# Projections of queries, keys and values as three passes over rounded and rest parts, in the causal and the self attention

## The chip, the cores and the metric

The kernel runs on one core of one Trainium2 chip. The metric is device time in microseconds (us) for one launch, the median of several runs; lower is better. TensorE (PE) multiplies matrices and writes to PSUM, VectorE (DVE) and ScalarE (ACT) compute element by element, GpSimd (POOL) does the same and issues DMAs, and SyncE (SP) issues DMAs.

## The reference

A decoder of two layers works on x, 4 sequences of 512 tokens and 256 features, in float32:

```python
x = x + _L0_attn_ref(_layernorm(x, axis=-1), ...)    # causal attention
x = x + _L0_xattn_ref(_layernorm(x, axis=-1), ctx_1024, ctx_1024, ctx_1024)   # gated gelu with the context
x = x + _L0_ffn_ref(_layernorm(x, axis=-1), ...)     # 8 experts, 2 a token, and a shared one
x = x + _L1_attn_ref(_layernorm(x, axis=-1), ...)    # self attention without a mask
x = x + _L1_xattn_ref(_layernorm(x, axis=-1), ctx_1024, ...)                  # cross attention
x = x + _L1_ffn_ref(_layernorm(x, axis=-1), ...)     # 8 experts, 2 a token
```

Each attention has 16 heads of 16 features. What the change touches is its first line:

```python
qkv = x @ W_attn.T + b_attn
q, k, v = jnp.split(qkv, 3, axis=-1)
```

The causal layer multiplies q and k by a factor of the position before the scores; the self attention of the second layer does not.

## The kernel before

The program runs five stages with a barrier between each: causal attention (names with `l0a`), gelu (`l0g`), experts (`l0m`), self attention followed by cross attention in one stage (`l1a`), experts (`l1m`). The change lies in `attention`, which both attention stages call.

`attention` works on batches (sequences) b = 0 to 3, and in `l1a` on 4 more of cross attention. A batch has 4 groups g of 4 heads, and a group has 8 steps j. One group is a slot (`self_slot`, L107). `attention_schedule` (L252) writes out a single list of steps for the whole stage, and each engine takes from the list the steps in which it has work, in that order. A step stands for an operation with a part on one or several engines:

- S: scores by key on PE (L959, and the mask at L929 in the causal layer), exponentials on ACT (L842). A: scores by query on PE (L920), row maxima on DVE (L729 causal, L734 self). Both share three PSUM buffers `s_ps` in turn, so PE waits when the reader of the buffer three turns back is not done.
- PV: probabilities by values on PE (L984). O, Z, N: the output of a group copied by ACT, turned by PE (L993), divided on DVE (L742, L746), turned back by PE (L1001) and copied by ACT (L859).
- M: row maxima turned by PE (L938) and copied by ACT (L811), for the group after.
- PREP with its EVAC, uses 0 to 7: the projections of the batch after, made one by one between the steps of this one. Uses 0 and 1 turn the normalised x (`xn`) with PE (L886), and ACT copies the result into `xnT` (L788). Uses 2 to 5 make the four 128-row chunks of queries and keys in the order `CHUNK` (L899), uses 6 and 7 the values (L906). Of queries and keys a rounded part `hi` and a rest `lo` are kept: the causal layer makes `qk` on DVE (L699), `hi` on ACT (L806) and `lo` on DVE (step LO, L716); the self attention makes both on DVE (L703, L705). ACT copies the values (L797).
- STACK, KEYS: DMAs that stack parts of `hi` and `lo` for the score products, issued by SP (L528), POOL (L608) and, for the first batch, ACT (L826).

Uses of later batches all go through one PSUM tile, `m_ps`, which N, M and the output projection (L1011) use too. `take_m` (L867) makes PE wait until whoever read `m_ps` last is done. For uses 0 and 1 this reader is named by `made` (L435): ACT's copy.

The first batch of a stage has nothing to hide behind. Its eight uses go through the three `s_ps` buffers ahead of the first slot, then the values and 8 A steps follow, and only then the first S:

```python
for use in range(8):
    yield "PREP", 0, use, 0
    yield "EVAC", 0, use, 0
    if 2 <= use < 6:
        yield "LO", 0, use, 0
    if use == 3:
        for g in range(2):
            yield "STACK", 0, g, 0
            yield from keys(0, g)
```

In the causal stage DVE's step LN2 of batch 0 ends with casts of constants, which wait for the DMAs of all seven constants (L678).

Of the kernel before, what the change touches and what calls it, by code (L numbers as in the profile page):

```python
# [19 lines left out]
F32 = mybir.dt.float32  # L20
# [8 lines left out]
P = 128  # L29
# [77 lines left out]
def self_slot(kinds, b, g):  # L107
# [12 lines left out]
    rests = {1: {0: 2, 2: 3}, 2: {2: 4, 5: 5}}.get(g, {})  # L120
    m_at = 5 if first else 3 if g in (1, 2) else 2
    turn_at = 5 if g == 0 else 6
# [172 lines left out]
def attention(nc, tag, x, const, stages):  # L295
# [12 lines left out]
    with ExitStack() as ctx:  # L308
# [18 lines left out]
        for n, (kind, w) in enumerate(stages):  # L327
            parts.append({"w": w, "kind": kind,
                          "wqkv": sb(f"wqkv{n}", [P, CC, 3 * D]), "wout": sb(f"wout{n}", [P, NG // 2, D]),
                          "bqk": sb(f"bqk{n}", [P, 2 * CC]), "bv": sb(f"bv{n}", [P, D]),  # L330
                          "bo": sb(f"bo{n}", [P, D]), "in": sem(f"w_in{n}")})

        def part(b):
            return parts[b // B]
# [4 lines left out]
        xn = sb("xn", [P, NT, D])  # L339
        xnT = sb("xnT", [P, CC, T])  # L340
        ctxT = sb("ctxT", [P, CC, T]) if has_cross else None
# [46 lines left out]
        m_act = steps("m_act", 4)  # L388
        m_dve = steps("m_dve", 4 if causal else 0)
        hi_done = steps("hi_done", 4)  # L390
        lo_done = steps("lo_done", 4)
# [102 lines left out]
        def in_stack(st, p, e, n):  # L494
            at = 64 * e + 16 * n
            return st[at:at + 16, p, :].bitcast(F32)

        block = ctx.enter_context(nc.Block())

        @block.sync  # L500
        def _(sp):
            def weights(n):
                w, at, loaded = parts[n]["w"], parts[n], parts[n]["in"]
                sp.dma_start(at["wqkv"][:, :, :], w["wqkv"].rearrange("(c p) n -> p c n", p=P)).then_inc(loaded, 16)
                sp.dma_start(at["bqk"][:, :], w["bqk"]).then_inc(loaded, 16)
# [61 lines left out]
        def _(pool):  # L567
            pool.memset(one_row[:, :].bitcast(F32), 1.0).then_inc(one_made, 1)

            def ln(b, *_):  # L570
# [13 lines left out]
                if b == 2 and has_cross:  # L584

                    w = parts[1]
                    pool.wait_ge(w["in"], 5 * 16)
                    for at in (w["wqkv"][:, :, 0:D], w["bqk"][:, 0:CC]):
                        pool.tensor_scalar(at, at, SCALE, None, ALU.mult).then_inc(q_scaled, 1)

            def bias(b, *_):

                if b % B == 0:
                    pool.wait_ge(part(b)["in"], 5 * 16)
                xn_done.wait(pool, b, NT - 1)
# [54 lines left out]
        def _(dve):  # L650
# [33 lines left out]
            def prep(b, use, _):  # L684
                if not 2 <= use < 6:
                    return
                if b % B == 0 and use == 2:

                    dve.wait_ge(part(b)["in"], 5 * 16)
                    if kinds[b] == "cross":  # L690
# [5 lines left out]
                if causal:  # L696
# [75 lines left out]
            def inverse_sums(b, g, kt):  # L772
                if kinds[b] != "cross":
# [5 lines left out]

            run({"LN1": ln, "LN2": normal, "EVAC": prep, "LO": rest, "ADD": out, "S": key_max, "W": inverse_sums,  # L780
                 "A": row_max, "Z": invert})

        @block.scalar
        def _(act):
            def prep(b, use, _):
                if use < 2:
                    m_ready.wait(act, b, use)
                    act.activation(xnT[:, use, :], product(b, use), ACT.Copy).then_inc(m_act.sem, 1)  # L788
                elif use >= 6:
# [9 lines left out]
                elif causal:  # L799
# [60 lines left out]

            run({"EVAC": prep, "S": exps, "O": copy_o, "M": negate_rows, "N": copy_back, "KEYS": first_stack})

        @block.tensor
        def _(pe):
            m_reader = [None]

            def take_m(steps, b, step):  # L867

                if m_reader[0]:
                    last, lb, lstep = m_reader[0]  # L870
                    last.wait(pe, lb, lstep)
                m_reader[0] = (steps, b, step)

            def prep(b, use, _):
# [13 lines left out]
                elif use < 6:  # L888
                    i = use - 2
                    if b % B == 0 and i == 0:  # L890
                        pe.wait_ge(w["in"], 5 * 16)
                        if cross:
                            pe.wait_ge(q_scaled, 2)
                    m_act.wait(pe, b, 1)
                    if cross and i == 1:
# [1484 lines left out]
```

## Time and profile before

| | |
|---|---|
| three runs | 1605.56, 1600.04, 1604.02 us, median 1604.02 |
| the profiled execution | 1612.28 us, of which the span from first to last instruction is 1610.5 |
| PE, matmuls | 1438.8 us busy, 89% of the span |
| DVE | 1176.1 us, 73% |
| ACT | 899.8 us, 56% |
| POOL | 612.2 us, 38% |
| causal attention | about 0 to 270 us of the span |
| self and cross attention | about 660 to 1190 us |

Busy time of PE counts from a matmul's start to its modelled end, and such spans overlap: what one matmul costs its successors is read from start to start. A float32 matmul appears as two records, a matmul of `float32r` operands (type F32R in the code) as one; the trace writes f32 for both. Numbers ahead of a row of the timeline are microseconds from the span's start.

### The profile page before, as it was taken

The numbers are of one execution on the slowest core, as the hardware profiler recorded it, in microseconds if no ns is written. First come the engines' busy times: TensorE is split into PE (matmuls) and PEld (weight loads), VectorE is DVE, ScalarE is ACT, GpSimd is POOL, SyncE is SP. The second block draws the span as 40 slices with busy tenths as digits, with TensorE's granted clock in tenths as the row PEclk, the third lists the DMA queues.
The fourth block names the chain that finished last, engine by engine and source line by source line (L and its number), as shares of the span: only waits on it lengthen the run. The fifth ranks groups of instructions, "written<-read, shape, count | busy, mean of one in ns | idle before, by whom it ended". The sixth has DMA issues, their size and how long they took to land. (4 is left out here: it accounts for less than half of the span.)

```text
span 1610.5 us, 30201 instructions
## 1 busy us (share of the span) xinstructions
PE 1438.8 (89%) x9918; PEld 994.5 (62%) x9918; DVE 1176.1 (73%) x2499; ACT 899.8 (56%) x1704; POOL 612.2 (38%) x881
## 2 busy tenths in 40 slices
PE   7899998989899999679999988999747899999996
PEld 3455554569899999333434333333236899999996
DVE  4776662554778888478878758988768688888883
ACT  1455553223256666036666687888814567776662
POOL 6445430010235654546445443553213223233311
PEclk8899998999999999769999999989978899999998
DMA  6223320130358886533223322232044678878772
GB/s 167 60 47 60 61 42 27 52 100 26 105 167 256 253 243 173 131 83 58 58 42 59 71 55 64 61 66 62 14 156 132 183 246 237 245 236 237 237 216 43
DMA packets 104553, 194.59 MB, mean 121 GB/s; under 512 B 30448, under 2 KB 55920, under 8 KB 101456
## 3 DMA queue, kind: packets, MB, share of 16 engines
q1 hardware_dynamic: 72016, 154.49, 30.8%
q0 software_dynamic: 31872, 37.79, 13.4%
q8 instruction: 79, 1.29, 0.3%
q14 instruction: 74, 0.61, 0.1%
q10 hardware_dynamic: 512, 0.40, 0.1%
HBM read 135.89 MB, written 18.61 MB: 96 GB/s over the span
## 5 line engine op out<-in xcount | busy, mean ns | idle before, releaser
L836 ACT ACTIVATE l1a_sb_probs<-l1a_s_ps,l1a_sb_kmax 128x512 f32<-128x512 f32 x256 | 172.4, 706 | 21.9 <-DVE l1a_sb_kmax L769 21.1
L734 DVE TENSOR_REDUCE l1a_sb_mx<-l1a_s_ps 128x2 f32<-128x1024 f32 x128 | 153.5, 1219 | 38.6 <-PE l1a_s_ps L920 38.5
L769 DVE TENSOR_REDUCE l1a_sb_kmax<-l1a_s_ps 128x1 f32<-128x512 f32 x256 | 161.0, 680 | 26.1 <-PE l1a_s_ps L959 25.2
L842 ACT ACTIVATE l1a_sb_probs<-l1a_s_ps 128x1024 f32<-128x1024 f32 x128 | 130.2, 1024 | 80.1 <-PE l1a_s_ps L959 79.9
L959 PEld LDWEIGHTS l1a_s_ps<-l1a_sb_qst,l1a_sb_kst 49*128 49x128 f32 (+1 forms) x512 | 49.1, 190 | 172.4 <-issue 95.3
L608 POOL DMA_DIRECT2D l1a_sb_kst<-l1a_sb_hi x228 | 112.9, 499 | 104.2 <-PE l1a_s_ps L959 96.2
L729 DVE CUSTOM_DVE_ANT_0 l0a_sb_seen<-l0a_s_ps,l0a_sb_above 128x128 f32<-128x128 f32 (+3 forms) x256 | 113.6, 488 | 52.5 <-PE l0a_s_ps L920 52.1
L2048 PE MATMUL l1m_g_ps<-l1m_sb_rows_hi,l1m_sb_hi 128*128 128x256 f32 x512 | 146.9, 287 | 1.1 <-DVE l1m_sb_late L1946 1.1
L959 PE MATMUL l1a_s_ps<-l1a_sb_qst,l1a_sb_kst 49*128 49x512 f32 (+1 forms) x512 | 127.5, 505 | 20.7 <-ACT l1a_sb_probs L836 18.9
L2048 PE MATMUL l1m_g_ps<-l1m_sb_rows_hi,l1m_sb_lo 128*128 128x256 f32 x512 | 145.3, 284 | 0.0
L2048 PE MATMUL l1m_g_ps<-l1m_sb_rows_lo,l1m_sb_hi 128*128 128x256 f32 x512 | 145.2, 284 | 0.0
L1781 POOL DMA_INDIRECT out_x<-l1m_sb_late,l1m_sb_add_to x39 | 64.9, 1663 | 192.2 <-DVE l1m_sb_late L1968 181.6
L1920 DVE TENSOR_TENSOR l1m_sb_lo<-l1m_sb_raw,l1m_sb_hi 128x512 fp32r<-128x512 f32 x184 | 119.8, 694 | 18.7 <-ACT l1m_sb_hi L1831 17.6
L842 ACT ACTIVATE l0a_sb_probs<-l0a_s_ps 128x1024 f32<-128x1024 f32 (+3 forms) x128 | 88.8, 702 | 63.7 <-PE l0a_s_ps L929 63.4
L2048 PE MATMUL l0m_g_ps<-l0m_sb_rows_hi,l0m_sb_hi 128*128 128x256 f32 x384 | 113.1, 294 | 7.1 <-DVE l0m_sb_rows_lo L1914 6.4
L2048 PE MATMUL l0m_g_ps<-l0m_sb_rows_hi,l0m_sb_lo 128*128 128x256 f32 x384 | 111.1, 289 | 0.0
L2048 PE MATMUL l0m_g_ps<-l0m_sb_rows_lo,l0m_sb_hi 128*128 128x256 f32 x384 | 111.1, 289 | 0.0
L1831 ACT ACTIVATE l1m_sb_hi<-l1m_sb_raw 128x512 fp32r<-128x512 f32 x184 | 104.9, 621 | 0.0
L2048 PE MATMUL l1m_y_ps<-l1m_sb_hi,l1m_sb_h_hi 128*128 128x256 f32 x312 | 91.9, 295 | 12.1 <-DVE l1m_sb_lo L1926 7.2
L2048 PEld LDWEIGHTS l1m_g_ps<-l1m_sb_rows_hi,l1m_sb_hi 128*128 128x128 f32 x512 | 98.8, 193 | 1.8 <-issue 1.5
L2048 PEld LDWEIGHTS l1m_g_ps<-l1m_sb_rows_hi,l1m_sb_lo 128*128 128x128 f32 x512 | 98.6, 193 | 0.1
L2048 PEld LDWEIGHTS l1m_g_ps<-l1m_sb_rows_lo,l1m_sb_hi 128*128 128x128 f32 x512 | 98.6, 193 | 0.0
(407 smaller groups left out, 3933.2 us busy)
## 6 DMA issues: line engine op xcount, KB each, us to landing
l1m_sb_raw<-in_l1m_w SPq DMA_DIRECT2D x92, 512.0 KB
l0m_sb_raw<-in_l0m_w SPq DMA_DIRECT2D x72, 512.0 KB
l1m_sb_raw<-in_l1m_w SPq DMA_DIRECT2D x23, 1024.0 KB
l1a_sb_qst<-l1a_sb_hi SPq DMA_DIRECT2D x256, 32.0 KB, 2.0
l1a_sb_kst<-l1a_sb_hi POOLq DMA_DIRECT2D x228, 32.0 KB, 2.0
l0a_sb_qst<-l0a_sb_hi SPq DMA_DIRECT2D x128, 32.0 KB, 2.3
l1a_sb_qst<-l1a_sb_lo SPq DMA_DIRECT2D x128, 32.0 KB, 2.1
l0a_sb_kst<-l0a_sb_hi POOLq DMA_DIRECT2D x124, 32.0 KB, 2.1
```

What stands on the lines that cost most here:

```text
L608: pool.dma_start(in_stack(kst, p, e, n), in_part(source, i, p, e)).then_inc(kstacked[p], 16)
L729: ins = dve.tensor_tensor_reduce(seen[:, j % 2, e, 0:last], buffer("A", b, g, j)[:, e, 0:last], above[:, T - last:T], 1.0, -3e38, ALU.add, ...
L734: dve.tensor_reduce(mx[:, g, qt, 2 * p:2 * p + 2], buffer("A", b, g, j)[:, :, :], AX.X, ALU.max).then_inc(a_max.sem, 1)
L769: dve.tensor_reduce(kmax[:, n % 4, e:e + 1], buffer("S", b, g, j)[:, e, :], AX.X, ALU.max, negate=True).then_inc(kmax_done.sem, 1)
L836: ins = act.activation(probs[:, n % 8, e, :], at[:, e, :], ACT.Exp, bias=kmax[:, n % 4, e:e + 1], accum_out=zsum[:, n % 4, e:e + 1])
L842: act.activation(probs[:, n % 8, :, c0:T], at[:, :, c0:T], ACT.Exp, scale=SCALE).then_inc(exp_done.sem, 1)
L959: ins = pe.matmul(at[:, e, c0:T], kst[rows, p, kt * P:(kt + 1) * P], qst[rows, p, c0:T], start=True, stop=not causal)
L1781: pool.indirect_dma_start(total, bass.IndirectOffsetOnAxis(ap=at, axis=0), y[:, e % 2, t, :], None, compute_op=ALU.add).then_inc(stored[e ...
L1831: ins = act.activation(two_chunks(hi, s % 2, f), raw13[:, s % n13, f, n, :, :], ACT.Copy)
L1920: ins = dve.tensor_tensor(two_chunks(lo, s % 2, f), raw13[:, s % n13, f, n, :, :], two_chunks(hi, s % 2, f).bitcast(F32), ALU.subtract)
L2048: ins = pe.matmul(at, s, m, start=n == 0, stop=n == len(passes) - 1)
```

## The change

The normalised and turned x is kept as a rounded part `x_hi` (ACT, in place of the copy into `xnT`) and a rest `x_lo` (DVE, a new step XLO). The weights of the causal and of the self attention are split once a stage into `w_hi` (ACT) and `w_lo` (DVE), in three pieces (step SPLIT: half of the query and key columns, the other half, the value columns). Each float32 product of these two layers becomes three float32r passes (hi by hi, lo by hi, hi by lo). Cross attention stays as it was. The weights' DMA gets a semaphore of its own. The reader of `m_ps` after uses 0 and 1 is now XLO instead of ACT's copy, and M moves from step 2 to step 3 in the slots of group 0.

```diff
-    m_at = 5 if first else 3 if g in (1, 2) else 2
+    turned_rests = {0: {4: 0, 5: 1} if first else {2: 0, 6: 1}}.get(g, {})
+    m_at = 5 if first else 2 if g == 3 else 3
@@
     for j in range(2 * NT):
         yield "S", b, g, j
+        if nxt is not None and kinds[nxt] != "cross" and j in turned_rests:
+            yield "XLO", nxt, turned_rests[j], 0
@@ def attention_schedule(kinds):
     yield "LN1", 0, 0, 0
     yield "LN2", 0, 0, 0
+    yield "SPLIT", 0, 0, 0
     for use in range(8):
         yield "PREP", 0, use, 0
         yield "EVAC", 0, use, 0
+        if use < 2:
+            yield "XLO", 0, use, 0
+        if use in (1, 4):
+            yield "SPLIT", 0, (use + 2) // 3, 0
         if 2 <= use < 6:
             yield "LO", 0, use, 0
@@ def made(b, use):
+            if use < 2 and kinds[b] != "cross":
+                return x_rest, b, use
@@ vector
+            def split_rest(_, k, __):
+                dve.wait_ge(w_split, k + 1)
+                dve.tensor_tensor(columns(w_lo, k), columns(parts[0]["wqkv"], k), columns(w_hi, k).bitcast(F32),
+                                  ALU.subtract).then_inc(w_rest, 1)
+
+            def turned_rest(b, use, _):
+                m_act.wait(dve, b, use)
+                v_ready.wait(dve, b - 1, 1)
+                dve.tensor_tensor(x_lo[:, use, :], product(b, use), x_hi[:, use, :].bitcast(F32), ALU.subtract
+                                  ).then_inc(x_rest.sem, 1)
@@ scalar
-                    act.activation(xnT[:, use, :], product(b, use), ACT.Copy).then_inc(m_act.sem, 1)
+                    at = xnT if kinds[b] == "cross" else x_hi
+                    act.activation(at[:, use, :], product(b, use), ACT.Copy).then_inc(m_act.sem, 1)
+            def split_weights(_, k, __):
+                act.wait_ge(parts[0]["wqkv_in"], 16)
+                act.activation(columns(w_hi, k), columns(parts[0]["wqkv"], k), ACT.Copy).then_inc(w_split, 1)
@@ tensor
+            def three_passes(at, chunks):
+                passes = [(s[a], m[b]) for s, m in chunks for a, b in ((0, 0), (1, 0), (0, 1))]
+                for n, (s, m) in enumerate(passes):
+                    ins = pe.matmul(at, s, m, start=n == 0, stop=n == len(passes) - 1)
+                return ins
@@ uses 2 to 5
+                    if not cross:
+                        if b == 0:
+                            pe.wait_ge(w_rest, 1 + i // 2)
+                        x_rest.wait(pe, b, 1)
+                        cols = slice(CHUNK[i] * P, (CHUNK[i] + 1) * P)
+                        ins = three_passes(at, [((w_hi[:, c, cols], w_lo[:, c, cols]), (x_hi[:, c, :], x_lo[:, c, :]))
+                                                for c in range(CC)])
@@ uses 6 and 7
+                    if b == 0:
+                        pe.wait_ge(w_rest, 3)
...
+                        if not cross:
+                            ins = three_passes(cols, [((x_hi[:, c, rows], x_lo[:, c, rows]),
+                                                       (w_hi[:, c, 2 * D:3 * D], w_lo[:, c, 2 * D:3 * D]))
+                                                      for c in range(CC)])
```

What DVE does for the first batch of the causal stage, before, from the end of LN2 to the first of the A steps (a row names line, operation, what is written and read, the shape, and how many follow):

```order
L682 CAST const_span_b<-l0a_sb_span 128x256
L699 SCALAR_TENSOR_TENSOR l0a_sb_qk<-l0a_s_ps,l0a_sb_bqk,const_rope 128x512
L716 TENSOR_TENSOR l0a_sb_lo<-l0a_sb_qk,l0a_sb_hi 128x512
L699 SCALAR_TENSOR_TENSOR l0a_sb_qk<-l0a_s_ps,l0a_sb_bqk,const_rope 128x512
L716 TENSOR_TENSOR l0a_sb_lo<-l0a_sb_qk,l0a_sb_hi 128x512
```

And in the changed kernel, whose line numbers are its own:

```order
L703 CAST const_span_b<-l0a_sb_span 128x256
L731 TENSOR_TENSOR l0a_sb_w_lo<-l0a_sb_wqkv,l0a_sb_w_hi 128x2x2x128
L737 TENSOR_TENSOR l0a_sb_x_lo<-l0a_s_ps,l0a_sb_x_hi 128x512 x2
L731 TENSOR_TENSOR l0a_sb_w_lo<-l0a_sb_wqkv,l0a_sb_w_hi 128x2x2x128
L720 SCALAR_TENSOR_TENSOR l0a_sb_qk<-l0a_s_ps,l0a_sb_bqk,const_rope 128x512
L748 TENSOR_TENSOR l0a_sb_lo<-l0a_sb_qk,l0a_sb_hi 128x512
L720 SCALAR_TENSOR_TENSOR l0a_sb_qk<-l0a_s_ps,l0a_sb_bqk,const_rope 128x512
L748 TENSOR_TENSOR l0a_sb_lo<-l0a_sb_qk,l0a_sb_hi 128x512
L720 SCALAR_TENSOR_TENSOR l0a_sb_qk<-l0a_s_ps,l0a_sb_bqk,const_rope 128x512
L731 TENSOR_TENSOR l0a_sb_w_lo<-l0a_sb_wqkv,l0a_sb_w_hi 128x2x256
```

Four subtractions stand behind the casts and ahead of the first `qk`, one more ahead of the third `lo`.

What ACT does at the same place, before:

```order
L806 ACTIVATE l0a_sb_hi<-l0a_sb_qk 128x512 x2
L826 DMA l0a_sb_kst<-l0a_sb_hi 16x512 x2
L826 DMA l0a_sb_kst<-l0a_sb_lo 16x512
L826 DMA l0a_sb_kst<-l0a_sb_hi 16x512 x2
L826 DMA l0a_sb_kst<-l0a_sb_lo 16x512
L806 ACTIVATE l0a_sb_hi<-l0a_sb_qk 128x512 x2
L797 ACTIVATE l0a_sb_v<-l0a_s_ps 128x512 x2
```

And in the changed kernel:

```order
L839 ACTIVATE l0a_sb_hi<-l0a_sb_qk 128x512 x2
L863 DMA l0a_sb_kst<-l0a_sb_hi 16x512 x2
L863 DMA l0a_sb_kst<-l0a_sb_lo 16x512
L863 DMA l0a_sb_kst<-l0a_sb_hi 16x512 x2
L863 DMA l0a_sb_kst<-l0a_sb_lo 16x512
L839 ACTIVATE l0a_sb_hi<-l0a_sb_qk 128x512
L843 ACTIVATE l0a_sb_w_hi<-l0a_sb_wqkv 128x2x256
L839 ACTIVATE l0a_sb_hi<-l0a_sb_qk 128x512
L830 ACTIVATE l0a_sb_v<-l0a_s_ps 128x512 x2
```

The rounding of the value weights stands behind the six DMA issues and the third `hi`.

What DVE does in group 0 of batch 1 of the self attention in the changed kernel, from step 2 on; before, the rows were the same without the two `x_lo`:

```order
L737 TENSOR_TENSOR l1a_sb_x_lo<-l1a_m_ps,l1a_sb_x_hi 128x512
L766 TENSOR_REDUCE l1a_sb_mx<-l1a_s_ps 128x2 x2
L774 RECIPROCAL l1a_sb_rz<-l1a_o_ps 128x16
L778 TENSOR_TENSOR l1a_sb_on<-l1a_o_ps,l1a_sb_rz 128x4x64
L766 TENSOR_REDUCE l1a_sb_mx<-l1a_s_ps 128x2 x2
L737 TENSOR_TENSOR l1a_sb_x_lo<-l1a_m_ps,l1a_sb_x_hi 128x512
L766 TENSOR_REDUCE l1a_sb_mx<-l1a_s_ps 128x2 x2
```

The second `x_lo` stands behind the maxima of steps 4 and 5. PE's turn back (N, L1001) stands at step 5, ahead of step 6, and takes `m_ps`, which this `x_lo` now frees.

## Rows read from the trace of the kernel before

**Rows 1.** Stretches by engine (busy us, records), granted clock, DMA share, GB/s

```profile
60.00:265.00 205.00, 192.31 (x1724) 102.59 (x1724) 130.29 (x510) 111.43 (x177) 85.10 (x162) 1.00 0.25 48
713.00:910.00 197.00, 188.75 (x1094) 77.44 (x1092) 159.60 (x197) 123.08 (x143) 90.63 (x167) 1.00 0.27 53
```

**Rows 2.** Waits of PE, 60 to 265 us: us, times, longest

```profile
PE l0a_s_ps L920 <- ACT l0a_sb_probs L842: 7.2, 12, 0.7
```

**Rows 3.** Timeline of PE: projection blocks and what follows them

```profile
716.10 1.98 PE L899 MATMUL l1a_m_ps<-l1a_sb_xnT,l1a_sb_wqkv 128*128 128x512 f32 x4
718.01 0.50 PE L959 MATMUL l1a_s_ps<-l1a_sb_qst,l1a_sb_kst 49*128 49x512 f32 x2
...
750.67 1.99 PE L906 MATMUL l1a_m_ps<-l1a_sb_wqkv,l1a_sb_xnT 128*128 128x256 f32 x8
752.60 0.50 PE L959 MATMUL l1a_s_ps<-l1a_sb_qst,l1a_sb_kst 49*128 49x512 f32 x2
```

**Rows 4.** Timeline of PE in the last expert stage, three-pass products

```profile
1287.23 0.28 PE L2048 MATMUL l1m_g_ps<-l1m_sb_rows_hi,l1m_sb_lo 128*128 128x256 f32 x1
1287.35 0.28 PE L2048 MATMUL l1m_g_ps<-l1m_sb_rows_lo,l1m_sb_hi 128*128 128x256 f32 x1
1287.47 0.40 PE L2048 MATMUL l1m_g_ps<-l1m_sb_hi,l1m_sb_rows_hi 128*128 128x512 f32 x1
1287.70 0.40 PE L2048 MATMUL l1m_g_ps<-l1m_sb_hi,l1m_sb_rows_lo 128*128 128x512 f32 x1
```

**Rows 5.** Timeline, start of the causal stage

```profile
10.99 1.06 PE L886 MATMUL l0a_s_ps<-const_ident,l0a_sb_xn 128*128 128x128 f32 x8 [1.55 <-DVE l0a_sb_xn L675]
12.88 8.80 PE L899 MATMUL l0a_s_ps<-l0a_sb_xnT,l0a_sb_wqkv 128*128 128x512 f32 x16 [0.83 <-ACT l0a_sb_xnT L788]
13.75 0.28 DVE L682 CAST const_span_b<-l0a_sb_span 128x256 bf16<-128x256 f32 x1
16.66 0.75 DVE L699 SCALAR_TENSOR_TENSOR l0a_sb_qk<-l0a_s_ps,l0a_sb_bqk,const_rope 128x512 f32<-128x512 f32 x1 [2.63 <-PE l0a_s_ps L899]
18.11 0.69 DVE L716 TENSOR_TENSOR l0a_sb_lo<-l0a_sb_qk,l0a_sb_hi 128x512 fp32r<-128x512 f32 x1 [0.70 <-ACT l0a_sb_hi L806]
21.52 3.62 PE L906 MATMUL l0a_s_ps<-l0a_sb_wqkv,l0a_sb_xnT 128*128 128x256 f32 x16
24.89 0.63 ACT L806 ACTIVATE l0a_sb_hi<-l0a_sb_qk 128x512 fp32r<-128x512 f32 x1 [4.77 <-issue]
27.06 0.33 PE L920 MATMUL l0a_s_ps<-l0a_sb_kst,l0a_sb_qst 48*128 48x128 f32 x2 [1.92 <-DVE l0a_sb_qk L699]
28.22 0.28 DVE L729 CUSTOM_DVE_ANT_0 l0a_sb_seen<-l0a_s_ps,l0a_sb_above 128x128 f32<-128x128 f32 x1
```

**Rows 6.** Timeline, start of the self attention

```profile
668.22 7.11 PE L899 MATMUL l1a_s_ps<-l1a_sb_xnT,l1a_sb_wqkv 128*128 128x512 f32 x16 [0.83 <-ACT l1a_sb_xnT L788]
670.29 0.75 DVE L703 TENSOR_SCALAR l1a_sb_hi<-l1a_s_ps,l1a_sb_bqk 128x512 fp32r<-128x512 f32 x1 [4.04 <-PE l1a_s_ps L899]
675.16 3.62 PE L906 MATMUL l1a_s_ps<-l1a_sb_wqkv,l1a_sb_xnT 128*128 128x256 f32 x16
677.28 0.61 ACTq L826 DMA_DIRECT2D l1a_sb_kst<-l1a_sb_lo  x1
678.71 1.25 PE L920 MATMUL l1a_s_ps<-l1a_sb_kst,l1a_sb_qst 48*128 48x512 f32 x6
679.25 9.14 DVE L734 TENSOR_REDUCE l1a_sb_mx<-l1a_s_ps 128x2 f32<-128x1024 f32 x8 [2.35 <-PE l1a_s_ps L920]
```

**Rows 7.** Timeline, group 0 of batch 1: the turn back and DVE's maxima

```profile
111.35 0.63 PE L1001 MATMUL l0a_m_ps<-const_ident,l0a_sb_on 128*128 128x128 f32 x4 [0.16 <-ACT l0a_sb_xnT L788]
111.92 0.08 DVE L729 DVE_READ_ACCUMULATOR2_ANT l0a_sb_mx<- 128x1 f32 x1
113.63 0.56 DVE L729 CUSTOM_DVE_ANT_0 l0a_sb_seen<-l0a_s_ps,l0a_sb_above 128x384 f32<-128x384 f32 x1 [1.62 <-PE l0a_s_ps L920]
...
771.61 2.35 DVE L734 TENSOR_REDUCE l1a_sb_mx<-l1a_s_ps 128x2 f32<-128x1024 f32 x2
772.70 0.63 PE L1001 MATMUL l1a_m_ps<-const_ident,l1a_sb_on 128*128 128x128 f32 x4
```

**Rows 8.** Stretches of the first slots, columns as in Rows 1

```profile
44.00:57.00 13.00, 11.25 (x62) 5.78 (x59) 10.08 (x44) 4.60 (x7) 4.36 (x5) 0.50 0.21 45
696.00:712.00 16.00, 12.68 (x46) 5.44 (x46) 14.84 (x24) 6.33 (x8) 6.65 (x6) 0.50 0.43 121
```

More of the change, by code:

```diff
@@ L339, in attention @@
         xn = sb("xn", [P, NT, D])
-        xnT = sb("xnT", [P, CC, T])
+        xnT = sb("xnT", [P, CC, T]) if has_cross else None
+        x_hi, x_lo = (sb(n, [P, CC, T], F32R) for n in ("x_hi", "x_lo"))
+        w_hi, w_lo = (sb(n, [P, CC, 3 * D], F32R) for n in ("w_hi", "w_lo"))
         ctxT = sb("ctxT", [P, CC, T]) if has_cross else None
@@ L389, in attention @@
         m_dve = steps("m_dve", 4 if causal else 0)
+        x_rest = steps("x_rest", 2, 0)
+        w_split, w_rest = sem("w_split"), sem("w_rest")
         hi_done = steps("hi_done", 4)
@@ L496, in in_stack, with columns @@
             return st[at:at + 16, p, :].bitcast(F32)
+        def columns(t, k):
+            if k == 2:
+                return t[:, :, 2 * D:3 * D]
+            return t[:, :, 0:2 * D].rearrange("p c (s h n) -> p c s h n", s=2, n=P)[:, :, :, k, :]
         block = ctx.enter_context(nc.Block())
@@ L586, in ln @@
                     w = parts[1]
-                    pool.wait_ge(w["in"], 5 * 16)
+                    pool.wait_ge(w["in"], 4 * 16)
+                    pool.wait_ge(w["wqkv_in"], 16)
                     for at in (w["wqkv"][:, :, 0:D], w["bqk"][:, 0:CC]):
@@ L593, in bias @@
                 if b % B == 0:
-                    pool.wait_ge(part(b)["in"], 5 * 16)
+                    pool.wait_ge(part(b)["in"], 4 * 16)
                 xn_done.wait(pool, b, NT - 1)
@@ L687, in prep @@
                 if b % B == 0 and use == 2:
-                    dve.wait_ge(part(b)["in"], 5 * 16)
+                    dve.wait_ge(part(b)["in"], 4 * 16)
                     if kinds[b] == "cross":
@@ L778, in inverse_sums @@
                 dve.reciprocal(rzsum[:, w % 2, :, :], zsum[:, n % 4:n % 4 + 2, :]).then_inc(rz_done.sem, 1)
-            run({"LN1": ln, "LN2": normal, "EVAC": prep, "LO": rest, "ADD": out, "S": key_max, "W": inverse_sums,
+            run({"SPLIT": split_rest, "XLO": turned_rest, "LN1": ln, "LN2": normal, "EVAC": prep, "LO": rest, "ADD": out, "S": key_max, "W": inverse_sums,
                  "A": row_max, "Z": invert})
@@ L901, in prep @@
                 else:
-                    src = ctxT if cross else xnT
+                    if b == 0:
+                        pe.wait_ge(w_rest, 3)
                     for t in (2 * (use - 6), 2 * (use - 6) + 1):
-                        cols = at[:, (t % 2) * D:(t % 2 + 1) * D]
+                        cols, rows = at[:, (t % 2) * D:(t % 2 + 1) * D], slice(t * P, (t + 1) * P)
+                        if not cross:
+                            ins = three_passes(cols, [((x_hi[:, c, rows], x_lo[:, c, rows]),
+                                                       (w_hi[:, c, 2 * D:3 * D], w_lo[:, c, 2 * D:3 * D]))
+                                                      for c in range(CC)])
+                            continue
                         for c in range(CC):
-                            ins = pe.matmul(cols, src[:, c, t * P:(t + 1) * P], w["wqkv"][:, c, 2 * D:3 * D],
+                            ins = pe.matmul(cols, ctxT[:, c, rows], w["wqkv"][:, c, 2 * D:3 * D],
                                             start=c == 0, stop=c == CC - 1)
```

9 lines of the change are left out of this document (5 added, 4 removed).

## The prediction

> **What bounds the kernel now.** I read the stretches by engine first, then the waits of PE, then the timeline at the three places that the change touches. In the two steady stretches of causal and self attention PE is busy 192.3 of 205 us and 188.8 of 197, at the full clock; DVE has 130.3 and 159.6 [rows 1]. What PE waits for there is mostly the exponentials, 7.2 us in 205 [rows 2]. So between the batches PE is the limit, and a microsecond taken from PE or added to it shows almost whole. Ahead of the first slot of either stage it is different: PE idles, and a chain over PE, DVE and ACT sets the time [rows 5, 6]. The change takes work from PE in the first kind of place and lengthens the chain in the second kind.
>
> **What PE saves between the batches.** A chunk of queries or keys is now a block of four records from 716.10 to 718.01, 1.91 us; a pair of value tiles is a block of eight, 750.67 to 752.60, 1.93 us [rows 3]. Within the value block the records follow each other at (1.99 - 0.38) / 7 = 0.23 us at most; over the sixteen at a stage's start it is (3.62 - 0.38) / 15 = 0.216, with 0.38 the modelled length of one [rows 3, 5]. The kernel has three-pass products already, in the experts: 0.23 us from start to start for 512 columns, 0.12 for 256 [rows 4]. The new blocks are 6 x 0.23 = 1.38 and 12 x 0.12 = 1.44 us. What comes on top for entering and leaving is 1.93 - 8 x 0.216 = 0.20 us in the old value block; the new one pays between nothing and that. So a chunk saves 0.33 to 0.53 and a value pair 0.29 to 0.49 us. Products in the experts follow each other without such a pause, but products of 48 and 49 rows stand beside these here, so I take nearer the low end: 0.38 and 0.32. There are 3 prepared batches x 4 chunks x 2 stages = 24 and 3 x 2 x 2 = 12. That is 9.1 + 3.8 = 12.9 us, with bounds of 11.4 and 18.6. PE's waits were 4 to 6% of the stretches, and some of the saving turns into such waits; I count 88%: **11.4 us gained**.
>
> The Trainium skill, page FP8 and Floating Point Precision, section TensorE Precision Notes, says that true float32 takes four passes through the array. By that alone a chunk would go from 8 passes to 6 and save a quarter of its 1.91 us, 0.48, and all 36 blocks 17 us: that is near my upper bound, where a pass for 256 columns costs 0.12 in rows and not half of 0.216.
>
> **What the start of the causal stage loses.** PE's first product now needs the rests of x and the first rest of the weights, all made by DVE, and DVE is held by the casts until 13.75 + 0.28 = 14.03 [rows 5]. Three subtractions stand ahead. One like them took 0.69 [rows 5]; those from PSUM may take 0.75, as L699 does. So PE starts at about 16.15 instead of 12.88. From start to reader the first product took 3.78 us, at the lower clock for most of it; with six passes in place of eight it is some 2.9. The first `qk` moves from 16.66 to about 19.05: 2.4 us. The chain behind it keeps its length, through the six DMA issues, to ACT's third `hi`: 24.89 becomes 27.3 [rows 5]. Now ACT adds 0.63 for the value weights behind it, DVE 0.69 behind that, and only then, at about 29.3, may PE make the values. Before, it made them from 21.52 in PE's idle time; now 24 passes stand on the path, 2.9 us at the full clock and 5.1 at half of it. The first A product, at 27.06 before, comes at 32.2 to 34.5, and DVE's first maximum, 28.22 before, at 32.6 to 34.9. The loss is 4.4 to 6.7 us. PE stands idle for about 5 us ahead of the value passes. After the shorter gap of 12.05 to 12.88 the sixteen records took 8.80 us where at the full clock they take 7.11 [rows 5, 6], so I expect the low clock in much of it: **6.0 us lost**. What waits behind (eight A steps, M, the rows' DMA, the first S) has no slack of its own, except POOL's issues, worth a few tenths.
>
> The Trainium skill, page TensorE: Matmul & The Clock Gate, section HAM oscillation, says that a pause of PE brings the clock back to half. By this rule the value passes start at half clock in both stages, which is the upper end of my two ranges, and the sum would be 6.7 + 6.0 - 11.0 = 1.7 us higher than mine. By that rule, the trace agrees: the pause ahead of 12.88 was followed by slow records [rows 5].
>
> **What the start of the self attention loses.** No casts stand here. The weights are fetched while the norm runs, x takes one more subtraction after ACT's second copy, and PE starts at about 669.0 instead of 668.22. The shorter product brings the first `hi` to 670.7 against 670.29 [rows 6]. After that DVE's pairs of 0.75 + 0.75 us set the pace, a little faster than the products did, and the second `lo` is 0.2 us late. ACT's issues end at 677.89 + 0.2 [rows 6]. Then ACT 0.63, DVE 0.69: 679.5. The values, made from 675.16 before, start there, and end at 682.5 or 684.7. DVE's first maximum moves from 679.25 to 683.1 to 685.2: 3.8 to 6.0 us, **5.0 lost**.
>
> **What the turn back loses.** In group 0 of batches 1 and 2 of either stage the second XLO is queued on DVE behind the maxima of steps 4 and 5, and PE's N at step 5 waits for it, with the value products and all later S and A queued behind N. Self attention: the maxima end at 771.61 + 2.35 = 773.96, a subtraction takes 0.69, so N starts at 774.7 instead of 772.70 [rows 7]; M's move lets DVE come some 0.2 us sooner, so 1.8. Causal: the last maximum ends at 112.0, N at 112.7 instead of 111.35: 1.35 [rows 7]. ACT and DVE have nothing to do meanwhile, since before as well DVE stood idle 1.62 us right after [rows 7]. Twice 3.15 is 6.3; some comes back as PE's later waits shrink: **6.2 lost**, bounds 4.0 and 7.0.
>
> **The rest.** In the first slot of either stage two subtractions stand between DVE's maxima. DVE is busy 10.1 of 13 us there in the causal stage, 14.8 of 16 in the other [rows 8]: 0.8 us lost in all, 0 to 2. The first XLO of the later slots, ACT's writing of `x_hi` (a copy as before) and the added semaphore cost nothing: before the maximum of step 3 DVE had room, and ACT is busy 111 of 205 and 123 of 197 us [rows 1]. The gelu, expert and cross stages keep their code.
>
> **The sum.** 6.0 + 5.0 + 6.2 + 0.8 - 11.4 = 6.6 us slower. The profiled execution took 1612.28 us, so the like of it would take 1618.9. That execution is 8.3 us above the median of the runs shown, 1604.02, so I forecast a median of **1610.6 us**. Differences under 0.3%, 4.8 us, can't be told from none.
>
> **The rivals.**
> - The costs outweigh the saving (0.60), as summed. Of this I put 0.50 above 4.8 us and 0.10 below.
> - Even (0.22): the blocks on PE enter and leave without a pause, so the saving is 0.88 x 18.6 = 16.4 us, and the clock does not fall before the value passes, so the starts cost 4.4 + 3.8. With 6.2 + 0.8 the sum is -1.2. For it: the experts' products follow each other at the bare 0.12 and 0.23 us. Against it: the pause of PE grows.
> - Faster (0.10): the clock of the first slots. Between 44 and 57 us and between 696 and 712 PE is busy 11.25 and 12.68 us at a granted clock of 0.50, the level of 1.2 GHz [rows 8]. If the shift of the start lets the clock rise at the head of these, where at half clock PE needs twice as long, up to half of 23.9 is given back where PE and not DVE is the limit. In the causal slot that is 5.6 us; half of the other, where DVE is busy 14.84 of 16, is 3. Sum: 6.6 - 8.6 = -2.0, and with the pauseless blocks of the case above -7 us, 1597. It decides from about 11 us of such returns on.
> - Slower by more (0.08): the clock falls in the new pauses and stays low for as long again as the 16 us at 696: some 8 us of PE's work in one stage, 1618 and above.
>
> So faster by over 0.3% 0.10, within 0.3% 0.32, slower 0.58. The range takes the even case and most of the faster one, and the upper bounds of the starts: 1601 to 1617.
>
> **What the profile after would show.** PE's chunk blocks near 1.5 us and value blocks near 1.6, from start to start. The first `qk` near 19, the first maximum at 33 to 35 us; in the other stage 4 to 6 us late. A wait of PE for `x_lo` ahead of the turn back, 1.3 us in the causal and 1.8 in the self attention, twice each. PE's busy share between the batches lower, its waits up by a few us. The forecast is wrong if the value passes of the first batch are hidden after all, if N finds `m_ps` free, or if the blocks shrink to 1.4 us.

## The result, and the profile after

The changed kernel takes 1618.1 us against 1604.8 us of the kernel before in the same comparison, medians of four runs each: ratio 1.0099, interval 1.0054 to 1.0143, so it is slower by 13 us, above the forecast range. Its profiled execution took 1618.47 us, at its own median, with a span of 1616.7.

The two profiled executions are only 6.2 us apart, though. What is missing of the 13 lies mostly in cross attention, whose code is unchanged. Here are its four batches, before and after, as stretches: us, busy PE, granted clock, DMA share, GB/s.

```profile
946.30:1002.40 56.10, 49.07 (x250) 0.94 0.23 49
1002.40:1055.90 53.50, 48.23 (x251) 0.97 0.30 67
1055.90:1110.50 54.60, 50.90 (x251) 0.91 0.31 68
1110.50:1157.00 46.50, 38.24 (x215) 0.93 0.16 32
```

```profile
962.40:1016.90 54.50, 48.63 (x250) 0.94 0.23 49
1016.90:1068.90 52.00, 46.77 (x251) 1.00 0.31 72
1068.90:1121.40 52.50, 48.05 (x251) 0.97 0.32 71
1121.40:1167.10 45.70, 37.17 (x217) 0.96 0.16 33
```

The same instructions took 210.7 us before and 204.7 after, since the clock fell more often in that execution of before. The last expert stage, unchanged too, was another 3 us shorter. So the forecast was right to subtract 8.3 us for a profiled execution above its median.

So the change is read from the starts of the same steps, after less before, in us, in this trace and in a second one of the same kernel (label again):

| place | first trace | second trace |
|---|---|---|
| first S of the causal stage | +6.17 | +6.56 |
| start of the stage after it | +6.6 | +6.7 |
| first A of self attention, counted from PE's last record of the stage before it | +6.1 | +6.0 |
| last self-attention batch, last slot | +16.2 | +16.5 |
| start of the last expert stage | +9.3 | +9.6 |

**Between the batches**, the stretches that answer to [rows 1]:

```profile
66.00:271.00 205.00, 187.82 (x1744) 108.07 (x1747) 133.13 (x516) 110.22 (x175) 84.84 (x162) 0.98 0.24 48
726.00:923.00 197.00, 183.93 (x1129) 82.58 (x1125) 159.32 (x198) 121.37 (x142) 90.37 (x167) 0.97 0.28 52
```

PE is busy 4.5 and 4.8 us less in stretches of the same length, though its blocks are shorter by about 10 us in all: the granted clock, 1.00 in both rows before, is 0.98 and 0.97, and what PE does then takes longer. Here are waits of PE in the first stretch and, as the third row, in 713 to 910 us (us in total, times, longest):

```profile
PE l0a_s_ps L977 <- ACT l0a_sb_probs L879: 8.1, 16, 1.0
PE l0a_m_ps L1058 <- DVE l0a_sb_x_lo L737: 3.1, 2, 1.6
...
PE l1a_m_ps L1058 <- DVE l1a_sb_x_lo L737: 4.0, 2, 2.0
```

The wait of N (L1058) for `x_lo` is there, twice in each stage. The timeline of PE at the first one in self attention answers to [rows 7], and the stretches behind three of the four show the clock:

```profile
785.99 0.63 PE L1058 MATMUL l1a_m_ps<-const_ident,l1a_sb_on 128*128 128x128 f32 x4 [2.01 <-DVE l1a_sb_x_lo L737]
786.55 1.28 PE L1041 MATMUL l1a_o_ps<-l1a_sb_probs,l1a_sb_vaug 128*32 128x512 f32 x8
787.76 0.79 PE L1016 MATMUL l1a_s_ps<-l1a_sb_qst,l1a_sb_kst 49*128 49x512 f32 x2
788.36 0.63 PE L977 MATMUL l1a_s_ps<-l1a_sb_kst,l1a_sb_qst 48*128 48x512 f32 x2
788.91 1.91 PE L1041 MATMUL l1a_o_ps<-l1a_sb_probs,l1a_sb_vaug 128*32 128x512 f32 x8
790.76 0.50 PE L1016 MATMUL l1a_s_ps<-l1a_sb_qst,l1a_sb_kst 49*128 49x512 f32 x2
```

```profile
786.00:791.00 5.00, 5.00 (x26) 0.66 0.00 0
851.00:860.00 9.00, 9.00 (x41) 0.62 0.00 0
179.00:184.00 5.00, 4.99 (x36) 0.66 0.01 1
```

Behind the pause of 2.01 us PE is busy without a gap, but eight value products take 1.91 us where 1.06 is usual. The clock went to the lower of its two levels, 1.2 GHz, for part of these stretches. That is a second price of the wait, and no term of the sum held it.

The clock fell once more in the causal stage, in its first batch: between 83 and 86 us it was granted at 0.69, and the chunk block that starts at 83.87 took 2.67 us. A wait of PE for a DMA, 1.09 us, ends at 81.74.

**The blocks.** A chunk of queries or keys is six records now; these are the first, the last and what follows [rows 3]:

```profile
733.10 0.50 PE L914 MATMUL l1a_m_ps<-l1a_sb_x_hi,l1a_sb_w_hi 128*128 128x512 f32 x1
...
734.36 0.39 PE L914 MATMUL l1a_m_ps<-l1a_sb_x_lo,l1a_sb_w_hi 128*128 128x512 f32 x1
734.68 0.50 PE L1016 MATMUL l1a_s_ps<-l1a_sb_qst,l1a_sb_kst 49*128 49x512 f32 x2
```

From start to start that is 1.58 us for 1.91, with some 0.1 us at either end over the 0.23 within. A value pair takes 1.62 us for 1.93. The saving is 0.33 and 0.31 us.

**The starts**, to be read beside [rows 5] and [rows 6]:

```profile
15.91 0.77 PE L914 MATMUL l0a_s_ps<-l0a_sb_x_hi,l0a_sb_w_hi 128*128 128x512 f32 x1 [4.00 <-DVE l0a_sb_x_lo L737]
18.94 0.75 DVE L720 SCALAR_TENSOR_TENSOR l0a_sb_qk<-l0a_s_ps,l0a_sb_bqk,const_rope 128x512 f32<-128x512 f32 x1 [2.57 <-PE l0a_s_ps L914]
27.71 0.61 ACT L843 ACTIVATE l0a_sb_w_hi<-l0a_sb_wqkv 128x512 fp32r<-128x512 f32 x1
28.35 0.69 DVE L731 TENSOR_TENSOR l0a_sb_w_lo<-l0a_sb_wqkv,l0a_sb_w_hi 128x512 fp32r<-128x512 f32 x1 [4.56 <-ACT l0a_sb_w_hi L843]
29.19 0.55 PE L914 MATMUL l0a_s_ps<-l0a_sb_w_hi,l0a_sb_x_hi 128*128 128x256 f32 x1 [6.00 <-DVE l0a_sb_w_lo L731]
33.87 0.50 PE L977 MATMUL l0a_s_ps<-l0a_sb_kst,l0a_sb_qst 48*128 48x128 f32 x4
34.24 0.29 DVE L761 CUSTOM_DVE_ANT_0 l0a_sb_seen<-l0a_s_ps,l0a_sb_above 128x128 f32<-128x128 f32 x1 [2.54 <-PE l0a_s_ps L977]
...
674.74 2.37 POOL L618 TENSOR_TENSOR x_sb<-x_sb,l1a_sb_bo 128x1024 f32<-128x1024 f32 x1 [2.70 <-DMA l1a_sb_wout<-in_l1a_wout]
675.43 2.23 DVE L731 TENSOR_TENSOR l1a_sb_w_lo<-l1a_sb_wqkv,l1a_sb_w_hi 128x512 fp32r<-128x512 f32 x1
677.59 0.74 DVE L724 TENSOR_SCALAR l1a_sb_hi<-l1a_s_ps,l1a_sb_bqk 128x512 fp32r<-128x512 f32 x1
686.06 0.55 PE L914 MATMUL l1a_s_ps<-l1a_sb_w_hi,l1a_sb_x_hi 128*128 128x256 f32 x1 [4.67 <-DVE l1a_sb_w_lo L731]
691.45 1.26 PE L977 MATMUL l1a_s_ps<-l1a_sb_kst,l1a_sb_qst 48*128 48x512 f32 x6
692.10 1.23 DVE L766 TENSOR_REDUCE l1a_sb_mx<-l1a_s_ps 128x2 f32<-128x1024 f32 x1 [4.73 <-PE l1a_s_ps L977]
```

The value passes wait for ACT's issues, its copy and DVE's subtraction, as forecast, and stand on the path: from their start to the first A it is 29.19 to 33.87 and 686.06 to 691.45, 4.68 and 5.39 us. In self attention all of them run at the lower clock (granted 0.50 from 686.0 to 691.4).

### The profile page after: what moved, and what is told of

Its sections match the earlier page's. It is cut to its first block and busy times, and to the rows that moved or that the text cites. A ratio compares the mean times of both kernels' runs of the same rounds, so it can differ in the third digit from the quotient of the medians.

```text
span 1616.7 us, 30501 instructions
## 1 busy us (share of the span) xinstructions
PE 1426.3 (88%) x10046; PEld 1012.3 (63%) x10046; DVE 1189.3 (74%) x2521; ACT 902.6 (56%) x1710; POOL 611.6 (38%) x881
## 3 DMA queue, kind: packets, MB, share of 16 engines
q8 instruction: 80, 1.31, 0.3%
## 5 line engine op out<-in xcount | busy, mean ns | idle before, releaser
L873 ACT ACTIVATE l1a_sb_probs<-l1a_s_ps,l1a_sb_kmax 128x512 f32<-128x512 f32 x256 | 172.5, 709 | 17.4 <-DVE l1a_sb_kmax L801 16.2
```

What stands on the lines that cost most here:

```text
L873: ins = act.activation(probs[:, n % 8, e, :], at[:, e, :], ACT.Exp, bias=kmax[:, n % 4, e:e + 1], accum_out=zsum[:, n % 4, e:e + 1])
```

## The experiments

My theory now, theory 1 in what was expected of the runs: the change loses by two chains, not by PE's work. One is the late split ahead of the first A of either stage. The other is N's wait, which costs its own length and then the clock. The rival is that the medians show something else than the traces, or that the loss is PE's smaller blocks being eaten by other waits.

**The same kernel again** (again), no edit.

> The changed kernel once more, unchanged, to see how large the change is beyond its first comparison. If the medians of the first runs are representative, it is 11 to 15 us above the kernel before (ratio 1.007 to 1.009). If the two profiled executions are (1612.3 and 1618.5), it is 5 to 8 us above (1.003 to 1.005). In the trace I expect the same steps at the same places: first maximum at 34.2 us, PE's wait ahead of the turn back of groups 0 some 1.3 to 2.0 us, and after most of these waits some 3 to 9 us at a granted clock of about 0.6 to 0.7.

1619.9 us against 1605.4, ratio 1.0091 (1.0062 to 1.0119): the medians of the first comparison stand. Waits ahead of N 1.57 us twice and 2.01 twice, as before to 0.01. The clock fell behind both of 2.01 and, other than in the first trace, behind none of 1.57.

**The second XLO a step earlier** (xlo_5).

```diff
-    turned_rests = {0: {4: 0, 5: 1} if first else {2: 0, 6: 1}}.get(g, {})
+    turned_rests = {0: {4: 0, 5: 1} if first else {2: 0, 5: 1}}.get(g, {})
```

> The second XLO of the later batches moves from step 6 to step 5 of group 0, ahead of the maxima of that step (1.22 us in self attention, 0.8 in the causal stage). Theory 1, the queue on DVE together with PE's clock: the pause of PE ahead of N shrinks from 1.6 and 2.0 us to 0.8 or less, the clock stays at 1.00 behind it, and the four turn backs, which cost about 12 us together, cost about 3: 8 to 9 us less than the changed kernel, about 1609. Rival, the queue alone: the clock falls all the same, and only the shorter wait is gained, 4 to 5 us, about 1613. If DVE's wait for ACT's copy delays the maxima, nothing is gained: 1617.

PE at the same place:

```profile
783.64 0.63 PE L1058 MATMUL l1a_m_ps<-const_ident,l1a_sb_on 128*128 128x128 f32 x4 [0.80 <-DVE l1a_sb_x_lo L737]
784.19 1.06 PE L1041 MATMUL l1a_o_ps<-l1a_sb_probs,l1a_sb_vaug 128*32 128x512 f32 x8
```

The pause is 0.80 us (0.89 in the causal stage), and the value products keep their 1.06. The last stage starts 8.4 us sooner than in the second trace of the changed kernel, as theory 1 said. The median did not come down to the 1609 expected: 1616.2 over four runs between 1607 and 1622, ratio 1.0081 (1.0056 to 1.0107). By itself it shows no gain; see the combination below.

**The value products of group 0 ahead of N** (n_after_pv), at step 5, with DVE's order untouched.

```diff
-        if j == turn_at and has_last and last[1] % 2:
+        if g and j == turn_at and has_last and last[1] % 2:
             yield "N", *last, 0
         if j in (5, 6):
             yield "PV", b, g, j - 5
+        if not g and j == turn_at and has_last and last[1] % 2:
+            yield "N", *last, 0
```

> DVE's order stays that of the changed kernel (the second XLO at step 6, behind the maxima of steps 4 and 5), but PE makes the first value products of group 0 (1.06 us) ahead of N and no longer behind it. So the queue on DVE is as long as in the changed kernel, and PE's pause is shorter by 1.06 us: 0.5 to 1.0 in place of 1.5 to 2.0. Theory 1, that PE's clock falls because of a pause of about 2 us: the clock stays at 1.00 behind all turn backs; 4.2 us from the pauses and 5 to 6 from the clock, 9 to 10 less than the changed kernel by the start of the last stage. Rival, that the clock falls for another reason (the load of these slots): 4 us less, with stretches at 0.6 to 0.7 as in the changed kernel.

```profile
783.78 0.63 PE L1060 MATMUL l1a_m_ps<-const_ident,l1a_sb_on 128*128 128x128 f32 x4 [1.02 <-DVE l1a_sb_x_lo L739]
784.33 0.50 PE L1018 MATMUL l1a_s_ps<-l1a_sb_qst,l1a_sb_kst 49*128 49x512 f32 x2
784.67 0.40 PE L979 MATMUL l1a_s_ps<-l1a_sb_kst,l1a_sb_qst 48*128 48x512 f32 x2
785.00 1.06 PE L1043 MATMUL l1a_o_ps<-l1a_sb_probs,l1a_sb_vaug 128*32 128x512 f32 x8
```

DVE's queue is as long as before, PE's pause 1.02 and 0.57 us, and the clock stays up behind all four. At the end of self attention the kernel is 9.2 us ahead of the second trace: theory 1 again. Some 6.5 of them are gone by the start of the last stage, in unchanged code. 1615.1 us, ratio 1.0043 (1.0020 to 1.0067).

**The pause alone, in the kernel before** (before_pause).

```diff
                 o_normed.wait(pe, b, g)
+                if g == 3 and b < 2:
+                    a_max.wait(pe, b + 1, 8 * 2 + 5)
                 take_m(oT_copied, b, g // 2)
```

> The kernel before, where the turn back of group 0 of batches 1 and 2 waits for the maximum of step 5 as well, which it does not need. No product, split or order is changed, so that only PE's pause is there: about 1.3 to 1.9 us in self attention, 0.7 or more in the causal stage. Theory 1, that a pause of this length costs the clock too: in self attention the step from the fifth to the sixth S grows from 2.40 to 4 us or more and the one behind it from 1.67 to about 3 with a granted clock below 1 behind the wait, 6 us in all; in the causal stage only the pause, 1.5 us in two. Rival, that the pause costs its own length alone: 1.3 to 1.9 us twice and the next steps as they were, 3 to 5 us in all.

The two turn backs of self attention:

```profile
783.27 1.04 PE L1003 MATMUL l1a_m_ps<-const_ident,l1a_sb_on 128*128 128x128 f32 x4 [1.46 <-DVE l1a_sb_mx L734]
784.23 1.94 PE L984 MATMUL l1a_o_ps<-l1a_sb_probs,l1a_sb_vaug 128*32 128x512 f32 x8
...
849.00 0.63 PE L1003 MATMUL l1a_m_ps<-const_ident,l1a_sb_on 128*128 128x128 f32 x4 [1.46 <-DVE l1a_sb_mx L734]
849.56 1.07 PE L984 MATMUL l1a_o_ps<-l1a_sb_probs,l1a_sb_vaug 128*32 128x512 f32 x8
```

After the same pause of 1.46 us the clock fell once and once not. The steps there grew by 2.9 and 1.3 us, in the causal stage (pauses of 0.92) by 0.76 each: 5.8 in all. The median is 6.9 us above the kernel before, ratio 1.0044 (1.0022 to 1.0067). So the wait costs several us without one three-pass product, and its second price comes at one place and not at the other.

Here are the turn backs of group 0 of batches 1 and 2 in all fourteen traces, by PE's idle time ahead of N; the clock is said to have fallen where the S steps behind N are longer than the pause explains:

| PE idle ahead of N | turn backs | clock fell behind |
|---|---|---|
| none to 0.16 us | 12 | 0 |
| 0.57 to 1.02 us | 14 | 0 |
| 1.46 us | 2 | 1 |
| 1.57 us | 14 | 5 |
| 2.01 us | 14 | 13 |

The length of the wait alone does not decide it. In the first batch of the causal stage ten traces show fifteen waits of PE, for exponentials or a DMA, of 0.98 to 1.09 us. Within 2.4 us behind four of them (in the two traces of the changed kernel, in combo and in combo_n, both below) the clock fell and one chunk block took 2.6 to 2.8 us; behind the other eleven it did not.

**The start: batch 0 in float32** (first_f32). Its products are float32 products of the unsplit tensors, as before the change. The weights are split behind them, ACT's part (SPLIT) ahead of the first A, DVE's (REST) behind the eighth maximum. The diff is cut: its other lines take SPLIT and XLO of batch 0 out of the old place and give its products `xnT` and the unsplit weights.

```diff
...
+    for k in range(3):
+        yield "SPLIT", 0, k, 0
     for j in range(2 * NT):
         yield "A", 0, 0, j
     yield "M", 0, 0, 0
+    for k in range(3):
+        yield "REST", 0, k, 0
...
```

> Batch 0 of each stage makes its products in float32 from the unsplit weights, as before the change; the weights are split once in the pause between the last value copy and the rows' first S (three ACT copies behind the value copies, three DVE subtractions behind the eighth maximum). Theory 1, that the start lost 6.1 us in each stage because the splits and the value passes stood on the path: both starts come back to those before the change, first maximum at 28.2 and, after the stage's start, 12 us less in sum: 1606, within 1 us either way. Rival, that the subtractions then hold DVE at the first slots, or that the clock falls elsewhere: 1609 to 1612.

The first A is at 26.65 us (27.06 before), in self attention 30.04 us behind the stage ahead of it (before 30.01, changed 35.96). The last stage starts 10.9 us sooner than in the second trace of the changed kernel. 1608.1 us, ratio 1.0022 (0.9999 to 1.0044). Both starts are back where they were before the change. By the two ratios they were worth 11 us of the 12 that theory 1 gave them, and the subtractions in the pause cost nothing that can be seen.

**The start: the value columns split earlier** (v_early).

```diff
-        if use in (1, 4):
-            yield "SPLIT", 0, (use + 2) // 3, 0
+        if use in (1, 3):
+            yield "SPLIT", 0, (use + 1) // 2, 0
```

> The value columns of the weights are split right behind the second chunk of the first batch, ahead of ACT's DMA issues, and no longer behind the fourth. Theory 1, that the value passes cost the start because they had to wait for ACT's issues, one copy and one subtraction: PE makes them while ACT issues, as before the change, and the first A product follows its stack. ACT's copy (0.63 us) now delays the issues instead. First maximum near 31.2 us in place of 34.2, and 3 us earlier in self attention too: 6 us less than the changed kernel. Rival, that the whole late start is the chain of x's rests and the first weights' rest: nothing changes, or it gets worse by 0.6 us a stage.

The first A comes 3.3 us sooner (30.94) and 3.1 us sooner (32.88 behind the stage ahead) than in the second trace. The ratio is 1.0045 (1.0021 to 1.0070) for 1.0091. So half of what either start lost came from the value passes' place behind ACT's issues.

**The start: PE kept busy** (warm_v): passes of ones ahead of the value passes, into a bank not yet used.

```diff
                     if b == 0:
+                        if use == 6:
+                            keep_warm(pe, o_ps[:, :], const, 24 if causal else 18)
                         pe.wait_ge(w_rest, 3)
```

> The changed kernel with 24 and 18 passes of ones into an unused bank ahead of the value passes of batch 0, so that PE does not idle for 6.0 and 4.5 us there. Theory 1, that the value passes run at half clock because of this pause: they take 2.9 us and not 4.7 and 5.4, and both starts come 1.8 to 2.5 us sooner, a little more where the maxima's products are then quick: 4 to 6 us less than the changed kernel. Rival, that the clock falls in spite of these passes, or that the passes themselves end later than the split: nothing gained, or up to 2 us lost.

The value passes of the causal stage, in this kernel and in the second trace of the changed one (busy us of PE, PE's weights, DVE, ACT, POOL; clock):

```profile
29.50:32.50 3.00, 3.00 (x24) 2.93 (x24) 1.90 (x3) 1.12 (x2) 3.00 (x7) 1.00 0.59 131
```

```profile
29.60:33.40 3.80, 3.80 (x18) 3.80 (x19) 1.78 (x3) 1.23 (x2) 3.46 (x8) 0.51 0.59 123
```

That is 24 passes in 3.00 us at clock 1.00 for 18 in 3.80 at 0.51: the pause was the cause of the slow passes. The first S comes 1.7 us sooner in the causal stage and 1.8 in self attention. The time, expected 4 to 6 us lower, does not follow: ratio 1.0110 (1.0082 to 1.0138). In the trace, against the second one of the changed kernel, 2.6 us are lost again by the end of the causal stage, 3.8 in the gelu and expert stages and 8.0 in cross attention, whose code is the same, and 2.3 are won back in self attention. I can't say whether the added work has to do with that.

**POOL's bias moved** (bias_late) behind its stack issues, for batch 0.

> The changed kernel with POOL's addition of the output bias (2.37 us) for batch 0 moved behind its stack issues, away from DVE's splits. Theory 1, that DVE's subtraction of two SBUF tensors took 1.61 and 2.23 us, and not 0.69, because POOL worked beside it: it takes 0.69, the first DVE reader of a product comes 0.2 to 0.9 us sooner in self attention, and the first maximum up to 0.9 us sooner; the causal stage stays. At most 1 us in all, so it shows in the trace and not in the time. Rival, that the subtraction is long for another reason: it stays over 1.5 us.

```profile
674.38 0.68 DVE L732 TENSOR_TENSOR l1a_sb_w_lo<-l1a_sb_wqkv,l1a_sb_w_hi 128x512 fp32r<-128x512 f32 x1
```

It takes 0.68 us, where the seven traces with POOL's addition (2.35 to 2.38 us) beside it show 1.61 to 2.23. But the first A comes 35.95 us behind the stage ahead of it, as before the edit: the copies and issues behind it set the pace. It explains nothing of the loss. The time, ratio 1.0142 (1.0103 to 1.0181), comes from four runs between 1616 and 1633, and its trace ends 1.4 us sooner than that of the changed kernel; I draw nothing from it.

**PE's saving taken back** (four_passes): float32 products of the rounded parts. This kernel makes the rests and leaves them out of the products.

```diff
-                passes = [(s[a], m[b]) for s, m in chunks for a, b in ((0, 0), (1, 0), (0, 1))]
+                passes = [(s[0].bitcast(F32), m[0].bitcast(F32)) for s, m in chunks]
```

> The products of queries, keys and values are float32 products of the rounded parts alone (the rest parts are still made and waited for, and left out of the products), so that only PE's time for each block goes back. If PE is the bound between the batches, each of 24 chunks costs 0.33 us more and each of 12 value pairs 0.30, 11.5 us, and the value passes of the two first batches about 1.5 us each: 1629 to 1633. The steps of the trace suggest that about 9 of the 11.5 were realised: 1628 to 1631. Rival, that waits for the exponentials and for the readers of the product buffer hide most of the saving: under 1624.

1635.6 us, ratio 1.0215 (1.0180 to 1.0250), 15.7 above the changed kernel and above the 1628 to 1633 expected. In the traces, against the second one of the changed kernel, 8.5 us of it stand at the last slot of self attention, and another 5.3 come in cross attention, with the same code. From step to step, the clock's part at the turn back left out, a batch costs 1.8 us more in the causal stage and 1.6 in self attention, of 4 x 0.33 + 2 x 0.31 = 1.94. So PE's saving is real and most of it shows; the rival falls.

**Both edits together** (combo: first_f32 and xlo_5).

> Both edits that paid: batch 0 of each stage in float32 with the split behind the first maxima, and the second XLO at step 5. By the starts of the stages in the two traces the first took 11 us off the changed kernel and the second 8; they touch other places, so together 19 us: 1598 to 1602, ratio 0.995 to 0.998. Rival, that they overlap (the clock of the first batch's slots stays low without the value passes' work ahead): 1604, no better than before.

1600.3 us, ratio 0.9966 (0.9947 to 0.9985): faster than the kernel before, as expected, and by the two ratios 9 us less than first_f32 alone, about what the earlier XLO was expected to be worth (8).

**And the value products ahead of N** (combo_n).

> As the one before, and PE makes the first value products of group 0 ahead of N. The wait that is left ahead of N, 0.75 us four times in two stages, is filled with work: 3 us less, 1595 to 1599, ratio about 0.995. Rival, that N's reader, and with it the copies on ACT and the second product, come later and cost as much: the same time as the one before.

```profile
765.81 1.06 PE L1053 MATMUL l1a_o_ps<-l1a_sb_probs,l1a_sb_vaug 128*32 128x512 f32 x8
766.80 0.66 PE L1070 MATMUL l1a_m_ps<-const_ident,l1a_sb_on 128*128 128x128 f32 x4
767.39 0.50 PE L1028 MATMUL l1a_s_ps<-l1a_sb_qst,l1a_sb_kst 49*128 49x512 f32 x2
```

No pause is left ahead of N. 1592.7 us, ratio 0.9916 (0.9886 to 0.9947): 14 us under the kernel before, and under the 1595 to 1599 expected. Against combo the four turn backs give 3.5 us, of 7.6 by the medians; the rest is not explained.

**That order in the kernel before** (before_n_after_pv).

> The kernel before with the first value products of group 0 ahead of N. In it PE hardly waits ahead of N, so there is nothing to fill: the step from the fifth to the sixth S stays at 2.4 us and the time within 0.2% of the kernel before. Then what the best version gains comes from the three-pass products, and not from this order. Rival: this order is better by itself, by 3 us or more.

Ratio 0.9996 (0.9976 to 1.0015); the step from the fifth to the sixth S is 2.20 and 2.25 us for 2.40. So the order alone gives nothing that can be measured in the time. The gain of combo_n is that of the three-pass products, once their two chains are gone: with the same order, its prepared batches are 1.4 to 1.7 us shorter than those of this kernel. In the traces the causal and self attention of combo_n are 10 us shorter than here and 12 us shorter than in the kernel before; what the median has beyond that comes from stages with the same code.

## Why the prediction was wrong

The direction was right, and each mechanism of the sum was seen; one that it lacked decided. The sum was 6.6 us. Measured were 13 to 14.5 by the medians, and 16 at the last slot of self attention. The median lay 7.5 us above the forecast and 1 above the range.

- **What the turn back loses** is the step that failed: "6.2 us lost, bounds 4.0 and 7.0". The pauses themselves were sized well: the S step at N grew by 1.4 us in the causal stage and by 2.0 in self attention where the clock stayed, 6.8 for four against 6.2. What was missing is the clock behind them. In the first trace the steps behind the waits grew by 3.0, 3.6 and 5.0 us where it fell, 13.0 in all with the fourth; in the second by 11.4. That is 5 to 7 us more than the term. The forecast had "the clock falls in the new pauses and stays low", but as a rival of 0.08, and it gave the value passes of the start, with a pause of 5 us, the lower clock while it gave N's pauses of 1.3 and 1.8 none. That rival named the measured time, 1618, with one low stretch as long as 16 us; the traces show two or three that end within 5 to 9 us.
- **The start of the causal stage**, 6.0: 6.2 and 6.6. First `qk` at 18.94 (19.05 forecast), third `hi` at 27.17 (27.3), value passes from 29.19 (29.3). Right.
- **The start of self attention**, 5.0: 6.0 to 6.1, its upper bound. All 24 value passes ran at the lower clock, which was that bound's reason. By the rule of the Trainium skill that the forecast weighed (TensorE: Matmul & The Clock Gate, HAM oscillation), this start should be at its upper end; the trace agrees, 5.39 us for the passes.
- **What PE saves**, 11.4: the blocks are shorter by 0.33 and 0.31 us, not 0.38 and 0.32, since the new block pays 0.2 us on entering and leaving as the old one did. 24 x 0.33 + 12 x 0.31 = 11.6, and at 1.8 and 1.6 of 1.94 us realised 10.2 at most; the causal stage's first batch, where the clock fell once, showed no saving. The table, without the starts and the steps at N, leaves 9.1 us in the first trace and 7.5 in the second for the saving less the first slots, where the forecast had 11.4 - 0.8 = 10.6. Off by 1.5 to 3 us. By the rule of the Trainium skill (FP8 and Floating Point Precision, TensorE Precision Notes) of four passes for true float32, a chunk would have saved 0.48 us; the measured 0.33 decides. Of the old 1.91 us 0.2 are paid either way, and a pass takes 0.23 us where an eighth of the old rest is 0.21.
- **The first slots**, 0.8: the traces do not separate it from the saving and the clock there.
- **The median against the profiled execution**: the subtraction was right. That 1618.9 us, forecast for a profiled execution like the one before, met 1618.47 is luck: the changed stages lost 10 us more than the sum, and the unchanged cross attention and last expert stage were 10 us shorter.
- Of the rivals, "even" and "faster" needed blocks without a pause and a high clock at the starts; neither came.

## What to carry to other kernels

- A new wait of the engine that bounds the kernel has two prices, its length and the clock behind it. Here a third of the pauses around 1.5 us and nearly all of 2 us had both, and now and then one of 1 us. Read the granted clock of the stretch behind such a wait, and put it into the sum and the range. Filling half of the pause with work that was next anyway (one step moved here) took the second price away.
- An operand that is prepared once, off the loop, can still stand on the path of the first use. Let the first use have the old form, and prepare the new one in a pause behind it.
- When a change that should pay does not, undo its side costs one by one before undoing it: here the same products went from 14 us slower to 14 us faster.

## What the runs showed of the hardware

- At the turn back the clock fell behind 13 of 14 pauses of 2.01 us, 5 of 14 of 1.57 us and none of 14 of 0.57 to 1.02 us, with PE over 90% busy in the stretches around them. In the first causal batch it fell behind 4 of 15 waits of 0.98 to 1.09 us. It then stayed low in part of the next 5 to 9 us. The same kernel shows both outcomes at the same place, so one trace isn't enough to price such a pause.
- DVE's subtraction of two SBUF tensors, 0.69 us by itself, took 2.23 and 1.61 us when it started 0.69 and 1.31 us behind POOL's addition: in both it ended 0.55 us after POOL did, and within 0.01 us of that in five more traces. The Trainium skill, SBUF — State Buffer, SBUF: two separate sides, says that the shared port pair is held for the whole instruction by whichever starts first and the other blocks; the traces agree.
- Stretches of unchanged code (the end of self attention and cross attention, 227 to 235 us) differed by up to 8 us between executions, with the granted clock.
